# Attention: GpSimd multiplies both pairs of probabilities before it splits weights, and VectorE takes the second sum one slot and beta two slots later

## What is computed

```python
sigma_q, sigma_k = elu(qq) + 1, elu(kk) + 1
scores  = where(causal, qq @ kk.T / scale, -inf)
att_dot = softmax(scores) @ vv
att_mem = sigma_q @ mem / (sigma_q @ z)
delta   = vv - sigma_k @ mem / (sigma_k @ z)
mem, z  = mem + sigma_k.T @ delta, z + sigma_k.sum()
att     = beta * att_mem + (1 - beta) * att_dot
out     = att @ Wo
```

## Time and profile before

| what | value |
|---|---|
| time, median of 3 runs | 690.46 us (689.67 to 691.1) |
| the profiled execution's own time | 688.85 us |
| its span, first to last instruction | 687.1 us |
| mean granted TensorE clock | 0.972 |
| TensorE matmul busy | 630.4 us, 92% |
| VectorE busy | 409.9 us, 60% |
| ScalarE busy | 332.6 us, 48% |
| GpSimd busy | 248.2 us, 36% |

### The profile page before, as it was taken

One profiled execution on the slowest core, in us unless ns is written; L12 is line 12 of the kernel. 1 busy time (PEld: TensorE's weight loads), 2 busy tenths in 40 slices (PEclk: granted clock), 3 DMA queues, 4 the chain that ended last, 5 costly groups with the idle time before them and its releaser, 6 DMA issues. The chain is left out here.

```text
span 687.1 us, 12129 instructions
## 1 busy us (share of the span) xinstructions
PE 630.4 (92%) x4182; PEld 551.5 (80%) x4182; DVE 409.9 (60%) x1047; ACT 332.6 (48%) x812; POOL 248.2 (36%) x283
## 2 busy tenths in 40 slices
PE   3999999999999999999999897688999958996997
PEld 2789889988989979989989796576777756985775
DVE  6849687388386388485484735694223279545444
ACT  2658677467577467576476551322444311201221
POOL 3718420156120167120120211606777505200474
PEclk9999999999999999999999999899999979996899
DMA  8101200001100000000000402794334270009541
GB/s 266 57 2 32 62 1 1 9 11 53 39 1 2 8 31 31 8 0 0 9 1 1 109 1 70 277 412 120 104 105 101 77 262 34 0 1 349 188 129 41
DMA packets 26513, 51.59 MB, mean 75 GB/s; under 512 B 4478, under 2 KB 15712, under 8 KB 26464
## 3 DMA queue, kind: packets, MB, share of 16 engines
q1 hardware_dynamic: 19456, 35.74, 15.1%
q0 software_dynamic: 4896, 13.12, 6.8%
q10 hardware_dynamic: 2112, 2.10, 0.9%
HBM read 41.76 MB, written 10.09 MB: 75 GB/s over the span
## 5 line engine op out<-in xcount | busy, mean ns | idle before, releaser
L907 DVE RECIPROCAL denominators<-readings 128x2 f32<-128x2 f32 x120 | 20.1, 167 | 113.4 <-PE readings L581 112.9
L786 ACT ACTIVATE memory_reading<-readings,denominators 64x128 f32<-64x128 f32 x240 | 73.8, 356 | 26.1 <-DVE denominators L907 24.6
L581 PEld LDWEIGHTS readings<-memory_copy,sigma 128*128 128x128 f32 x480 | 70.6, 191 | 9.5 <-ACT memory_copy L777 1.7
L591 PE MATMUL memory<-minus_delta,sigma_k_tokens 128*128 128x129 f32 x480 | 75.0, 278 | 3.5 <-DVE minus_delta L913 3.4
L468 POOL TENSOR_TENSOR scores<-scores,score_max 128x512 f32<-128x512 f32 x16 | 16.7, 1045 | 168.2 <-DVE score_max L928 168.2
L581 PE MATMUL readings<-memory_copy,sigma 128*128 128x129 f32 x480 | 73.7, 275 | 1.6 <-ACT memory_copy L777 1.6
L913 DVE SCALAR_TENSOR_TENSOR minus_delta<-readings,denominators,v 64x128 f32<-64x128 f32 x224 | 69.0, 348 | 4.0
L591 PEld LDWEIGHTS memory<-minus_delta,sigma_k_tokens 128*128 128x128 f32 x480 | 63.2, 191 | 6.3 <-DVE minus_delta L913 5.0
L777 ACT ACTIVATE memory_copy<-memory 128x258 f32<-128x258 f32 x120 | 46.9, 391 | 42.5 <-PE memory L591 42.3
L630 PE MATMUL ahead<-wo,attT 128*128 128x256 f32 x256 | 64.9, 398 | 1.2 <-DVE attT L942 1.2
L1217 POOL DMA_INDIRECT xs_e<-rows_e,gather_at_e x46 | 44.6, 970 | 52.1 <-DVE gather_at_e L1631 18.2
(11 more groups left out here) (288 smaller groups left out, 1466.2 us busy)
## 6 DMA issues: line engine op xcount, KB each, us to landing
weights_e<-experts SPq DMA_DIRECT2D x24, 608.0 KB, 12.0
xn<-L_attn_Wq SPq DMA_DIRECT2D x4, 512.0 KB, 3.9
wo<-L_attn_Wo SPq DMA_DIRECT2D x1, 2048.0 KB, 13.2
rows_e<-xn ACTq DMA_DIRECT2D x4, 512.0 KB, 9.4
xn<-L_attn_Wv SPq DMA_DIRECT2D x3, 512.0 KB, 3.9
xn<-L_attn_Wk SPq DMA_DIRECT2D x3, 512.0 KB, 3.8
x<-L_attn_x SPq DMA_DIRECT2D x4, 256.0 KB, 4.0
x<-L_attn_x SPq DMA_DIRECT2D x2, 512.0 KB, 3.7
```

Source lines behind the costliest of these rows:

```text
L581: last = pe.matmul(KQ[g][:, hh * MC:(hh + 1) * MC], sqk[:, GROUP * g + hh, pair, 2 * par:2 * par + 2, :], mz[g][:, hh, :], start=True, sto ...
L591: last = pe.matmul(MM[g][:, hh * MC:(hh + 1) * MC], skt[:, GROUP * g + hh, pair, :], dl[g][par][:, hh, :], start=False, stop=True, skip_gr ...
L786: last = act.activation(read[rows, half, GROUP * g + hh, pair, :], KQ[g][rows, hh * MC:hh * MC + DK], ACT.Copy, scale=nr[g][rows, hh:hh + 1])
```

## The change

GpSimd now does the probabilities of both pairs first, in every stage with a wait for its own first pair in between, and then all three splits. VectorE takes the second sum in slot 8 (after that slot's sigma) and beta in slot 9.

```diff
                         probabilities(n, 0, before)
-                        if not (half or last):
-                            pool.wait_ge(p_ready, 4 * n + 2)
-                            split_next(it, 0)
+                        pool.wait_ge(p_ready, 4 * n + 2)
                         probabilities(n, 1)
                         if not (half or last):
                             pool.wait_ge(p_ready, 4 * n + 4)
-                            split_next(it, 1)
-                            split_next(it, 2)
+                            for place in range(3):
+                                split_next(it, place)
...
-                    if m in (5, 7):
-                        sum_exp(n, m // 7)
-                    if m == 7 and not half:
+                    if m in (5, 8):
+                        sum_exp(n, m // 8)
+                    if m == 9 and not half:
                         set_beta(it)
```

## The result

The changed kernel takes **682.27 us** (median of 4 runs, 680.95 to 683.57) against 690.43 (4 runs, 689.67 to 691.1): a ratio of 0.9883 with a 95% interval of 0.9862 to 0.9905, 8.2 us faster.

A forecast was written before the change was run, and what follows sets the result against it. TensorE was taken to bound stages 1, 3, 5 and 6, late VectorE to stall 0, 2 and 4. Terms 2.0 + 2.0 + 0.9 = 4.9 us off the 690.46 median gave 685.6 us, range 684.2 to 688.4.

The forecast's parts named there:

- Stage 0's term: Stage 0, stall at sigma_k's turn in slot 13, hanging on slot 12's sigma: 0.9 us gained, bounds 0 and 1.08.
- Slot 9's lateness: Stages 2 and 4: slot 9's beta and lengthened sigma make VectorE 1.4 us late at worst, covered by 2.7 us of room.
- C: Last split of stage 0 runs late, delaying stage 1's shift by 0 to 2.5 us: 688.1 us, chance 0.08.
- about at the stage's end: Sign that the forecast is right: the Wk split ends about at the end of its stage.
- Other stages: Stages 1, 3, 5 and 6 have at most 0.11 us each of TensorE idle to give; stage 7 gives 0.
- The term of stages 2 and 4: Both stalls before the updates of slots 9 and 10 go: 2.0 us a stage, 4.0 for both.
- The lower bound of the range: All marked loss, 5.2 us, about 0.8 of run spread and 0.2 for the odd stages: 684.2 us.
- B: VectorE's sigmas in stages 2 and 4 stay slow without a split beside them: gain 1.3 us, 689.1 us; B and E together 0.11.
- D: Collisions move to slots 10 to 12 of stages 0, 2 and 4, losing 2.9 us a stage: 694.4 us, chance 0.04.

The follow-up runs named there:

- the finer split: Changed kernel with beta left in slot 7 and every weight split in 16 smaller GpSimd instructions instead of 8: 690.47 us, ratio 1.0021 against before.

## Why the forecast missed

**The mechanism was right.** Stages 2 and 4 lost their time to VectorE's lateness in slots 8 and 9, which came from a split beside the sigmas and a sum and beta ahead of a step; the two steps came within 0.06 us of where the forecast put them. Either part of the change alone ends both stalls, and with beta back in slot 7 they stay away. Stage 0's term, 0.9, measured 0.87, in part by luck: its stall fell by 0.91 us, from 1.08 to 0.17, but slots 9 and 10 gave another 0.26 that was not forecast, and slot 14's local product took back 0.31. Slot 9's lateness was hidden, as costed: the forecast's worst, 156.6, is 154.5 in the new frame, and the step came at 153.86. The Wk split, forecast near 86.5 in stage 0, ended at 85.41 with a start 0.9 earlier, so C was missed by 0.3 us; the finer split shows that its price is real. The sign "about at the stage's end" contradicted that 86.5 and did not come: the Wk split ended 9.0 us into the next stage in stage 0 and 3.6 in stage 2. In C the sum of stage 2 ends at 153.4, by the working of slot 8 at 152.55; nothing hung on it.

**The term "Other stages" failed.** I wrote that stages 1, 3, 5 and 6 are TensorE's own length, that nothing on another engine can shorten them, and that they have at most 0.11 us each to give. They gave 0.33 + 0.41 + 0.41 + 0.29 = 1.44 us, all of it from VectorE's order, which ends the meeting of slot 8's sigma and the second probabilities. The forecast had worked this out for stages 2 and 4 and not for the others, where the sigma takes 2.09 us in stage 3 and 1.91 in stage 6. The reading that failed is that of the earlier trace rows: length less busy time was taken for all that a stage can lose. Busy time of pipelined matmuls is modelled, and a start that is late by 0.1 or 0.2 us hides in the modelled length of the one before.

**The term of stages 2 and 4 was too small for the same reason.** Stage 6 was the yardstick, 5.67 us from turned probabilities to local product, and itself lost 0.23 there: 5.44 is left. The gain is 2.19 and 2.22, not 2.0; with it the sum is 6.72, not 4.9. The lower bound of the range was built from marked losses and inherited the error.

**The rest is scatter.** 690.43 - 6.72 is 683.7, below the range by itself and still 1.4 above the measured median; the repeat gave 6.9 us. The time ahead of the first scores and the clock after the attention move a run by about that much, and the 0.8 us that I allowed for it was thin.

**The rivals.** B was priced wrongly: it kept slot 8's long sigma, whose cause, the second probabilities, the change itself moves behind the sum. D did not come about in the changed kernel at its price: its sign, idle time before sigma_k's turns, is there with 0.17 us in stage 0 and 0.22 in stages 2 and 4, and VectorE's part alone brings out 0.7 to 1.4. The prediction argued that a reordering only moves collisions, and then D was to be feared. They did move, to slots 9 to 11, where VectorE has room, and some went: VectorE is busy 34.90 us in stage 2 and 30.85 in stage 3 before, 33.52 and 30.96 in the changed kernel.

## What to carry to other kernels

When GpSimd lengthens VectorE's instructions, look for the slots in which that engine has room and move the GpSimd work there; where the order can't be changed, cutting its instructions finer can do as much, as it did here, as long as the cut work itself is nowhere waited for. A stage without marked idle time is not yet at its floor: before a stage serves as a yardstick, compare the distance between two starts with the shortest such distance anywhere in the kernel. When a work item is moved behind the end of a stage, check the in-order engine that meets it there: here 0.3 us were left.

## What the runs showed of the hardware

GpSimd's multiplication for the split costs 0.58 us an instruction of 128x256 beside a quiet VectorE (2.33 for 4) and 0.36 us for 128x128 (2.90 for 8): half the work is not half the time.

The part after the seven stages has the same instructions in all kernels here and took from 307.0 to 309.6 us, with a mean granted clock of 0.95 down to 0.92. That is a mean of two levels: in the changed kernel, for one, 540 to 548 us has 1.00 (2.4 GHz) with TensorE busy 4.71 of the 8 us, and 548.4 to 555 has 0.50 (1.2 GHz). Two such windows, of the changed kernel and of the one with GpSimd's part alone:

```profile
372.18:679.20 307.02, 267.87 (x1539) 221.79 (x1538) 159.22 (x432) 88.96 (x225) 126.53 (x130) 0.95 0.40 133
```

```profile
374.21:683.40 309.19, 274.00 (x1539) 228.00 (x1538) 158.86 (x432) 88.95 (x225) 126.25 (x130) 0.92 0.40 132
```

Of the change only stage 7's later sum lies in it, and there the last wait for ScalarE's result ends 34.8 us after stage 7's first scores in both. The clock does not follow the edits: the changed kernel's repeat had 308.4 us, at 0.93. This is why differences under 2 us were read here from the stages, in which the granted clock is 1.00, and not from the times.
